# Row maxima in pairs: two products and one 1024-column maximum per step, and three pairs of the second head placed ahead of the attention

## The reference, cut to what matters

```python
def _mha(q, k, v, heads=8):                       # d = 80
    scores = jnp.einsum('bhqd,bhkd->bhqk', qh, kh) * d ** (-0.5)
    probs = jax.nn.softmax(scores, axis=-1)
    out = jnp.einsum('bhqk,bhkd->bhqd', probs, vh)
...
query = hidden_states @ Wq                        # (2, 1024, 640)
keyt, valt = enc @ Wk, enc @ Wv                   # enc: (2, 2044, 384)
hs = _mha(query, keyt, valt)
ca_q1 = einsum(ca, Wq_ca)[:, indices, :]          # ca: the last 4 rows of the context
ca_hs1 = _mha(ca_q1, residual, residual)
ca_hs2 = _mha(ca_hs1 @ Wq, ca @ Wk_ca, ca @ Wv_ca)
out = (hs + ca_hs2) @ Wout + b_out + residual
```

## Time and profile before

| | us |
|---|---|
| median of 3 runs | 1210.48 (1210.38 to 1210.54) |
| the profiled execution, device time | 1210.61 |
| its span in the profile | 1208.8 |
| PE busy | 1195.8 (99%) |
| DVE busy | 823.3 (68%) |
| ACT busy | 681.8 (56%) |
| POOL busy | 206.3 (17%) |

### The profile page before, as it was taken

How to read it: one execution, slowest core, us unless ns; L and a number is a source line. 1 busy time by engine, 2 the same in 40 slices (tenths; PEclk the granted TensorE clock), 3 DMA queues, 4 the chain that set the end, 5 groups by cost and what they waited for, 6 DMA issues and landing times.

```text
span 1208.8 us, 14556 instructions
## 1 busy us (share of the span) xinstructions
PE 1195.8 (99%) x5640; PEld 905.3 (75%) x5640; DVE 823.3 (68%) x1177; ACT 681.8 (56%) x784; POOL 206.3 (17%) x119
## 2 busy tenths in 40 slices
PE   7999999999999999999999999999999999999999
PEld 6888888787666677777777777777777777776899
DVE  6458625771144388888888888888888888885552
ACT  5322433222644467677677677677777777778310
POOL 0100000010000011221221221221221221221233
PEclk9999999999999999999999999999999999999999
DMA  8974785593910074344344445335335325421254
GB/s 301 348 272 177 256 304 209 221 322 116 301 34 1 1 197 99 108 118 111 109 115 104 115 111 130 101 99 141 99 90 153 89 86 151 129 73 66 78 207 152
DMA packets 77935, 178.08 MB, mean 147 GB/s; under 512 B 14169, under 2 KB 31705, under 8 KB 74026
## 3 DMA queue, kind: packets, MB, share of 16 engines
q1 hardware_dynamic: 70106, 156.29, 42.7%
q0 software_dynamic: 2864, 10.24, 2.6%
q10 hardware_dynamic: 4896, 10.62, 2.5%
HBM read 113.72 MB, written 63.24 MB: 146 GB/s over the span
## 4 chain that ended last, share of the span: by engine, by line
PE 98%; DVE 1%; DMA 0%; ACT 0%; issue 0%; DVEq 0%; ACTq 0%
PE at_ps L1298 30%; PE bank L697 20%; PE at_ps L1279 19%; PE at_ps L233 9%; PE acc_t_ps L1062 7%; PE at_ps L1487 6%; PE s_ps L1030 2%; PE bank L644 1%; PE bank L674 1%; PE acc_t_ps L1041 1%; PE f_ps L233 1%; PE f_ps L983 1%; PE f_ps L993 0%; DMA ctx_f<-in_ctxT 0%; PE at_ps L1490 0%; PE f_ps L1004 0%
## 5 line engine op out<-in xcount | busy, mean ns | idle before, releaser
L249 DVE TENSOR_REDUCE mpart<-at_ps 128x1 f32<-128x512 f32 x480 | 324.7, 685 | 102.2 <-PE at_ps L233 102.1
L1218 ACT ACTIVATE prob_hi<-at_ps 128x1024 fp32r<-128x1024 f32 (+1 forms) x256 | 263.1, 1028 | 189.3 <-PE at_ps L1279 189.3
L1298 PE MATMUL at_ps<-prob_hi,v 128*81 128x512 f32 (+1 forms) x1024 | 317.1, 395 | 0.2 <-issue 0.2
L1155 DVE TENSOR_TENSOR prob_lo<-probs,prob_hi 128x1024 fp32r<-128x1024 f32 (+1 forms) x211 | 271.2, 1285 | 20.8 <-ACT probs L1223 20.3
L1223 ACT ACTIVATE probs<-at_ps 128x1024 f32<-128x1024 f32 (+1 forms) x256 | 260.9, 1019 | 0.0
L1298 PEld LDWEIGHTS at_ps<-prob_hi,v 128*81 128x81 f32 (+1 forms) x1024 | 150.5, 149 | 69.6 <-issue 6.2
L1155 POOL TENSOR_TENSOR prob_lo<-probs,prob_hi 128x1024 fp32r<-128x1024 f32 x45 | 108.1, 2403 | 512.5 <-ACT probs L1223 512.5
L233 PE MATMUL at_ps<-a 128*128 128x512 f32 x480 | 188.4, 393 | 0.4 <-DVE mpart L249 0.4
L1279 PE MATMUL at_ps<-b 113*128 113x512 f32 (+1 forms) x512 | 161.2, 396 | 0.0
L1279 PE MATMUL at_ps<-a 128*128 128x512 f32 (+1 forms) x512 | 160.3, 394 | 0.2 <-DVE vw L936 0.2
L1298 PE MATMUL at_ps<-prob_lo,v 128*81 128x512 f32 (+1 forms) x512 | 160.2, 394 | 0.0
(11 more groups left out here) (153 smaller groups left out, 1383.7 us busy)
## 6 DMA issues: line engine op xcount, KB each, us to landing
v_hi_d<-v_t SPq DMA_DIRECT2D x16, 648.0 KB, 5.9
v_lo_d<-v_t SPq DMA_DIRECT2D x16, 648.0 KB, 7.1
v<-v_hi_d SPq DMA_DIRECT2D x16, 648.0 KB, 4.8
v<-v_lo_d SPq DMA_DIRECT2D x16, 648.0 KB, 6.1
k_hi_d<-out_hi SPq DMA_DIRECT2D x40, 256.0 KB, 5.1
k_lo_d<-out_lo SPq DMA_DIRECT2D x40, 256.0 KB, 5.8
a<-k_hi_d SPq DMA_DIRECT2D x16, 640.0 KB, 7.7
b<-k_hi_d SPq DMA_DIRECT2D x16, 640.0 KB, 11.4
```

What stands on the lines that cost most here:

```text
L249: dve.tensor_reduce(self.mpart[:, g % 2, qt, c:c + 1], at[:, 0:w], AX, ALU.max).then_inc(self.mx_done, 1)
L1155: eng.tensor_tensor(pl[n % PB][0:r, :], prob[n % PF][0:r, :], ph[n % PB][0:r, :].bitcast(F32), ALU.subtract).then_inc(sem, 1)
L1218: act.activation(ph[n % PB][0:r, :], s_ps[n % 2][0:r, :], ACT.Exp, scale=SCALE).then_inc(ph_done, 1)
L1298: mm = pe.matmul(o_ps[:, u * CH:(u + 1) * CH], a[0:r, t, :], y[n % PB][0:r, u * CH:(u + 1) * CH], start=t == 0 and m == 0, stop=t == KT - ...
```

## The change

A step now does two pieces. `score_piece` makes two products into both banks of the buffer and signals once, with the second; `max_piece` takes one maximum over 1024 columns. A query tile has two pairs instead of four pieces, so `MXN` is 16 and a head has 17 steps. There is one buffer of two banks: before pair `n` PE waits until maximum `n - 1` is done. The last chunk, which was 508 columns, is now 512 that begin four columns earlier, so that both halves are whole.

In a usual tile slot 0 is empty and the pair stands in slot 1. In the tile with the row, the row stands in slot 1 and the pair in slot 2. DVE makes `split(n + 1)` first and the maximum behind it; only where slot 0 is filled (one tile, `n = 6`) one maximum comes first.

In the token attention a step of head 0 stands at every other `k` (24, 26, ... 56), and three pairs of head 1 follow at `k` = 58, 60 and 62 (`AHEAD`). The other 13 pairs of head 1 take the first 12 tiles of the attention.

```diff
-MXN = ST * SKV // CH
+MXP = SKV // CH // 2
+MXN = ST * MXP
 STEPS = MXN + 1
-FIRST_PIECES = (2, 3, 2, 3, 3, 2, 3, 3, 2, 3, 3, 3)
+AHEAD = 3
+FIRST_PIECES = (1, 1, 1, 1, 1, 1, 2, 1, 1, 1, 1, 1)
-SPLIT_AT = 1
...
     def score_piece(self, pe, mx_ps, g, k):
         n = g * STEPS + k
-        to = mx_ps[n % 2]
         if k == 0:
             self.a_loaded(pe, g)
-        if n >= 2:
-            pe.wait_ge(self.mx_done, n - 1)
+        if n:
+            pe.wait_ge(self.mx_done, n)
         if k < MXN:
-            qt, c = divmod(k, SKV // CH)
-            w = min(CH, SK - c * CH)
-            pe.matmul(to[:, 0:w], self.queries_a(g)[:, qt * P:(qt + 1) * P], self.keys_a(g)[:, c * CH:c * CH + w],
-                      start=True, stop=True).then_inc(self.mx_full, 1)
+            qt, half = divmod(k, MXP)
+            for u in range(2):
+                first = min((2 * half + u) * CH, SK - CH)
+                mm = pe.matmul(mx_ps[:, u, :], self.queries_a(g)[:, qt * P:(qt + 1) * P],
+                               self.keys_a(g)[:, first:first + CH], start=True, stop=True)
+            mm.then_inc(self.mx_full, 1)
...
     def max_piece(self, dve, mx_ps, g, k):
...
-            dve.tensor_reduce(self.mpart[:, g % 2, qt, c:c + 1], at[:, 0:w], AX, ALU.max).then_inc(self.mx_done, 1)
+            qt, half = divmod(k, MXP)
+            dve.tensor_reduce(self.mpart[:, g % 2, qt, half:half + 1], mx_ps.rearrange("p u n -> p (u n)"), AX, ALU.max
+                              ).then_inc(self.mx_done, 1)
...
         def maxima(k):
             k -= MAX_FROM * pairs
-            return [k] if 0 <= k < STEPS else []
+            return [divmod(k // 2, STEPS)] if k >= 0 and k % 2 == 0 and k // 2 < STEPS + AHEAD else []
...
-            pe.wait_ge(at.mx_done, STEPS)
+            pe.wait_ge(at.mx_done, STEPS + AHEAD)
             fold_values(0)
...
 def pieces(n):
     if n < KT - EARLY:
-        return [(1, k) for k in range(sum(FIRST_PIECES[:n]), sum(FIRST_PIECES[:n + 1]))]
+        some = [(1, AHEAD + k) for k in range(sum(FIRST_PIECES[:n]), sum(FIRST_PIECES[:n + 1]))]
+        return [None] + some if len(some) == 1 else [some[0], None, some[1]]
     g, t = divmod(n + EARLY, KT)
-    each = MXN // KT
-    rows = [None, (g, MXN)] if t == 0 and g < G else []
-    return rows + ([(g + 1, each * t + k) for k in range(each)] if g + 1 < G else [])
+    rows = [(g, MXN)] if t == 0 and g < G else []
+    return [None] + rows + ([(g + 1, t)] if g + 1 < G else [])
...
-                first = SPLIT_AT if todo and todo[0][1] < MXN else 0
+                places = pieces(n)
+                todo = [piece for piece in places if piece]
+                first = 1 if places and places[0] else 0
```

More of the change, by code:

```diff
@@ L238, in score_piece @@
             pe.wait_ge(self.neg_done, g + 1)
-            pe.matmul(to[0:ST, 0:P], self.mneg[:, g % 2, :], self.eye[:], start=True, stop=True
+            pe.matmul(mx_ps[0:ST, 0, 0:P], self.mneg[:, g % 2, :], self.eye[:], start=True, stop=True
                       ).then_inc(self.mx_full, 1)
@@ L754, in tokens @@
         r2 = s.sb("r2", [P, B, KC * NH])
-        f_ps = [s.psum(f"f_ps{i}", [P, CH]) for i in range(2)]
+        f_both = s.psum("f_ps", [P, 2, CH])
+        f_ps = [f_both[:, i] for i in range(2)]
         s_ps = [s.psum(f"s_ps{i}", [P, 2, CH]) for i in range(2)]
@@ L959, in vector @@
                 n, j = divmod(k, pairs)
-                for m in maxima(k):
-                    at.max_piece(dve, f_ps, 0, m)
-                    if m == MXN - 1:
+                for g, m in maxima(k):
+                    at.max_piece(dve, f_both[:], g, m)
+                    if (g, m) == (0, MXN - 1):
                         at.top(dve, 0)
@@ L1064, in tensor @@
                 mm.then_inc(pv_done, 1)
-                for m in maxima(k):
-                    if m == 0:
+                for g, m in maxima(k):
+                    if (g, m) == (0, 0):
                         pe.wait_ge(wk2_done, B)
-                    at.score_piece(pe, f_ps, 0, m)
+                    at.score_piece(pe, f_both[:], g, m)
                 for group in FOLD_AT.get(k, ()):
@@ L1106, in pieces @@
     if n < KT - EARLY:
[L1107 removed]
+        some = [(1, AHEAD + k) for k in range(sum(FIRST_PIECES[:n]), sum(FIRST_PIECES[:n + 1]))]
+        return [None] + some if len(some) == 1 else [some[0], None, some[1]]
     g, t = divmod(n + EARLY, KT)
[L1109 to L1111 removed]
+    rows = [(g, MXN)] if t == 0 and g < G else []
+    return [None] + rows + ([(g + 1, t)] if g + 1 < G else [])
 def attend(nc, outer, kept, at, wout, tokens_end, d, scratch):
[L1117 removed]
+    assert AHEAD + sum(FIRST_PIECES) == MXN == KT and len(FIRST_PIECES) == KT - EARLY
     folded_values, gathered, last_gather, last_copy = tokens_end
@@ L1132, in attend @@
         s_ps = [wide[i][:].rearrange("p u n -> p (u n)") for i in (2, 0)]
-        mx_ps = [wide[1][:, i] for i in range(2)]
+        mx_ps = wide[1][:]
         o_ps = wide[3][0:DA].rearrange("p u n -> p (u n)")
@@ L1250, in vector @@
                 g, t = divmod(n, KT)
-                todo = [piece for piece in pieces(n) if piece]
-                first = SPLIT_AT if todo and todo[0][1] < MXN else 0
+                places = pieces(n)
+                todo = [piece for piece in places if piece]
+                first = 1 if places and places[0] else 0
                 for h, k in todo[:first]:
```

8 lines of the change are left out of this document (2 added, 6 removed).

## The result

The changed kernel takes 1230.57 us (median of 5 runs, 1230.36 to 1230.86), the kernel before 1210.48 on the same chip: ratio 1.0166, interval 1.0154 to 1.0177. It is 20.1 us slower. The prediction had the sign and said 1222.6, at most 1227.5: too little by 8 us, and outside its range. The profiled execution has a span of 1229.0 us for 1208.8.

What follows compares the result with a forecast made beforehand. The prediction took PE, busy for 99% of the span, to bound the kernel. Its terms, 8.0 + 3.2 + 1.0 - 0.3 + 0.2 = +12.1 us on the median of 1210.5, gave 1222.6 us, range 1213.5 to 1227.5.

Steps and rivals of the forecast that it cites:

- What bounds the kernel: Whole kernel: PE bounds it, busy for 99% of the span, 0.233 us a product with no room for a wait.
- part 2: Products: wider ones cost 0.2 us; six move from the first 12 tiles to the token attention, 1.4 us, net 0.
- A: Rival, products: the pitch falls, some 2,900 products gain 0.005 us each, 14 us, giving 1208.6 us; chance 7%.
- D: Rival, signals of the maxima's products: they cost PE time, 240 fewer save 4.8 us, giving 1217.8 us; chance 5%.
- Part 1: Maximum of 1024 columns on DVE: takes 1.22 us, saves 0.15 us a pair, some 36 us, none on PE's path.
- Rival C: Rows, heads' starts, early waits: the large maximum costs 1.37 us, 4.4 us more, giving 1227.0 us; chance 10%.
- Covered, by half a microsecond: Token attention, last head 1 pair: maximum ends 2.2 us after the pair began, PE rewrites its banks at 2.7 us.
- Part 3: One buffer in the usual tile: DVE fits `split` and maximum within 2.79 us, slack 0.8 us, no wait, cost 0.
- Part 4: Tile with the row: the pair waits for DVE's copy of the row, 0.57 us in 14 tiles, 8.0 us.
- Rival B: Tile with the row: the copy costs nothing, DVE does it before `split` or PE stays occupied; 1214.6 us, chance 12%.
- Part 5: End of a head: emptying slot 0 costs 0.232 us, 3.2 us for 14; next pair's wait 0.07 us, 1.0 us.
- Part 6: First 12 tiles of the attention: old waits of 1.2 us go, new ones of 0.9 us come, together -0.3 us.

## Why the prediction was wrong, point by point

**What bounds the kernel, and part 2's pitch**: right. PE's pitch is 0.23 us in both kernels, and in the kernel before, DVE's subtractions shortened by 14 us in all moved nothing. Rivals A and D (a faster pitch, costly signals) are out: the twelve tiles of a head that have no wait last 2.78 us on average in both kernels, 0.05 us less a head with half the signals, where A asked for 0.9 us a head and D for 0.3. What rival D quotes of the Trainium skill (TensorE: Matmul & The Clock Gate, section The cost: per-tile semaphore tail) is stated there for small products packed side by side into the array, which run at the same time; here the products start 0.23 us apart. Sixteen signals a head at its 26 ns would be 0.42 us, an estimate from that page, and the trace does not show it.

**Part 1**: the maximum's 1.22 us was right, its saving of 0.15 us a pair was not. The experiment with two maxima gives 0.06. DVE's busy time fell by 6.4 us, not 36. The records of the maxima did shrink by 38 us, summed over both traces, but records of neighbours overlap, and 14 of the 51 us of such overlap went too; and the blocked subtractions cost 18 (211 of 1372 ns for 1285), 12 of them in the collision with the multiplication. Against the kernel with two maxima (831.8 us) the large one saves 15. Rival C, 1.37 us, took its price from the same wrong addition.

**Part 2, the token attention**: the products were right (1.4 us in, 1.4 us out, shown by the run without them). Mis-sized was what lies beside them. "Covered, by half a microsecond" was asked only of the last pair. Head 0's maxima stand ahead of DVE's fold, and ACT and PE wait for that, as far as the waits tell: 0.75 us more at `wq_place` and 0.23 us at the last fold. +1.2 us, of which the list of waits names 1.0.

**Part 3, "Cost 0": this is the step that failed.** It gave DVE 1.22 us of `split` and 1.22 us of maximum in 2.79, and a slack of 0.8 us, from one tile in which POOL did nothing. In iteration 16 g + 10 POOL's multiplication blocks the subtraction for 1.8 us. DVE idles 0.5 us ahead of a usual maximum (110.7 us in 237), the slack takes up 0.8 to 0.9, and the remaining 0.4 us with the 0.10 behind a late product is the cost: +0.50 us in 14 heads, 7.0 us. Taking the multiplication away or cutting it in four gave 7.0 and 7.1 us back; cutting it in the kernel before gave nothing. The last sentence of the prediction named this sign, "waits in tiles without a row", as the one that would prove it wrong.

**Part 4**: the mechanism and the place of the copy were right to 0.01 us; the term was 0.64 us, not 0.57, because PE starts 0.15 us after the copy's end here and not 0.06: the delay was read from a product that waits for one semaphore, and this pair waits for two (that this is the cause is not shown). 14 x 0.64 = 9.0 for 8.0 us, and well within the bounds of 0.3 to 0.75. Rival B fell with it: even with the copy first, 0.28 us of the wait stay.

**Part 5**: right in both terms. 0.23 and 0.09 us against 0.232 and 0.07; the kernel before with late pieces showed 3.7 us for 3.2 in the whole and the 0.23 us in each tile.

**Part 6**: right in its sum. The first 16 tiles changed by -1.01 us; without the products (-1.4) and part 4's row (+0.64) that is -0.25, for -0.3. Tile 6 waits 0.38 us for a forecast of 0.4. The second pair does wait for its maximum (0.38 us of idle at 428.95), where 0.5 was said.

**The sum**, mended: 12.1 + 7.0 (part 3) + 1.2 (part 2) + 1.0 (part 4) + 0.3 (part 5), less 0.7 for the other tiles, which are 0.05 us a head shorter, and less 0.2 for the wider products, which no tile shows, makes 20.7. The spans differ by 20.2; the projections, which the change leaves alone, ended 0.5 us earlier in this execution. The range missed because all its bounds were about sizes of costs that I had found, and none about a place that I had not looked at.

## What to carry to other kernels

When a change takes slack away (one buffer for two, a longer instruction ahead of a wait), one usual tile does not show whether it was needed: list the group of each instruction on that engine and look at the longest ones, not the mean, since a delay hidden by the slack shows only as a long record. The length of that record is not yet the cost: count from where it ends to where the next engine needs the result. Merging two maxima that ran back to back saved 0.06 us of 1.28 here, not the 0.15 us that two single records suggest, and whoever waits for the merged one waits for all of it. And where an engine waits for another once in each stage, move independent work of the same count into that wait: the only version that beat the kernel before did just that.

## What the runs showed of the hardware that was not expected

- A subtraction of DVE with both inputs in SBUF stands still while POOL's multiplication runs: 1.22 us became 2.17 in the kernel before and 3.02 after, ending 1.08 and 1.09 us after POOL's instruction. In all 15 collisions of the kernel before and all 25 after, the end is 1.07 to 1.09 us behind POOL's, wherever the subtraction began. POOL's in four parts of 256 columns costs it 0.13 and 0.39 us, while the four take 3.81 us for 2.40 in one; the part that came second lasts 1.72 us for 0.73 and ends 0.60 us after the subtraction. DVE's maxima over PSUM are not slowed: 57 of them begin beside an instruction of POOL in the kernel after, and last 1.22 or 1.23 us.
- Two 512-column maxima back to back take 1.28 us, one of 1024 columns 1.22, while a single one has a record of 0.68.
- A product that had to wait for the copy of the row started 0.15 us after its end in all 14 tiles of the changed kernel and again in the 14 with the copy first, but 0.06 us in the kernel before; the 15 products that PE's list has waiting for a maximum started 0.055 to 0.057 us behind it. Those with 0.15 us wait for a second semaphore too, long satisfied, the others for one. No run takes the second wait away, so that this is the cause is not shown.
